# A four-layer graph network: one column of 128 edges per pair of nodes, fetched from the pair's first edge

## The reference

```python
edge_index = stack([src, dst])
h = relu(layernorm(x)); x = x + L0(h)   # relu(batchnorm(sums of (h@W)[src]*dinv[src]*dinv[dst] over dst + own + bias))
h = relu(layernorm(x)); x = x + L1(h)   # q.k attention over the edges of a dst, with e = edge_attr(10)@We
                                        # added to k and v; + h@Wskip; relu, batchnorm
h = relu(layernorm(x)); x = x + L2(h)   # sums over the edges of a src of edge_weight*h[dst]; @W.T + b
h = relu(layernorm(x)); x = x + L3(h)   # sums over the edges of a dst of h[src]; @W; + h@W_self
```

## Time and profile before

| | |
|---|---|
| median of the runs (lowest, highest) | 5445.5 us (5443.48, 5448.52) |
| span of the profiled execution | 5449.7 us |
| TensorE, VectorE, ScalarE, GpSimd busy | 4724.4, 3769.9, 2201.9, 2090.5 us |
| stages: preparation | 0 to 266.6 |
| layer 0's loop | 266.6 to 1120.1 |
| end of layer 0, layer norm, queries | 1120.1 to 1254.8 |
| attention's fetches | 1254.8 to 3533.0 |
| end of layer 1, layer norm | 3533.0 to 3686.6 |
| layer 2 (products of H end) | 3686.6 to 4709.6 |
| layer norm, split, transposes | 4709.6 to 4775.6 |
| layer 3's loop | 4775.6 to 5384.1 |
| the rest | 5384.1 to 5449.7 |

### The profile page before, as it was taken

The page is one execution under the profiler, slowest core; times in us unless marked ns, Lnnn a source line. Parts: engine busy times, 40 slices in busy tenths (PEclk is TensorE's granted clock), DMA queues, the critical chain, the costliest instruction groups (busy, mean ns, idle before and its releaser), DMA issues.

```text
span 5449.7 us, 102910 instructions
## 1 busy us (share of the span) xinstructions
PE 4724.4 (87%) x38199; PEld 3405.6 (62%) x38199; DVE 3769.9 (69%) x6411; ACT 2201.9 (40%) x4109; POOL 2090.5 (38%) x2152
## 2 busy tenths in 40 slices
PE   1299999957888898898889888859999999699997
PEld 0276666735777777777777777725555554356665
DVE  4888888837777777777777777739999997710001
ACT  0166666654555555555555555541222220200000
POOL 4212211006777777777777777700000000001110
PEclk6599999978999999999999999979999999899998
DMA  8156665527888888888888888837888887456664
GB/s 220 64 183 204 215 204 192 178 90 201 216 216 220 217 215 218 220 214 218 217 216 215 212 220 213 212 126 252 296 295 293 299 299 304 180 180 203 208 204 129
DMA packets 1235894, 1154.95 MB, mean 212 GB/s; under 512 B 466847, under 2 KB 1148819, under 8 KB 1206019
## 3 DMA queue, kind: packets, MB, share of 16 engines
q1 hardware_dynamic: 779992, 802.55, 45.9%
q10 hardware_dynamic: 367917, 193.82, 12.6%
q0 software_dynamic: 87488, 151.98, 11.8%
HBM read 691.95 MB, written 468.81 MB: 213 GB/s over the span
## 4 chain that ended last, share of the span: by engine, by line
PE 45%; SPq 18%; POOL 15%; issue 8%; DVE 8%; DMA 3%; ACT 2%; DVEq 0%; POOLq 0%; ACTq 0%
PE psum L1409 44%; POOL G L838 7%; POOL H L838 7%; SPq L629 4%; DVE R L861 4%; SPq L626 3%; SPq L632 3%; SPq L510 2%; SPq L637 2%; DMA H<-local_dst_pairs 1%; ACT H L1727 1%; DVE H L861 1%; SPq L488 1%; SPq L618 1%; POOL R L789 1%
## 5 line engine op out<-in xcount | busy, mean ns | idle before, releaser
L1727 ACT ACTIVATE HT<-psum 98x512 f32<-98x512 f32 (+2 forms) x1527 | 980.0, 680 | 373.5 <-PE psum L1409 307.8
L1409 PE MATMUL psum<-R,HT 128*128 128x384 bf16 x6076 | 1084.9, 326 | 3.8 <-DVEq L1398 3.8
L1727 ACT ACTIVATE H<-psum 128x512 f32<-128x512 f32 (+1 forms) x765 | 455.9, 597 | 1465.5 <-PE psum L1631 774.2
L1409 PE MATMUL psum<-R 128*128 128x98 bf16 (+3 forms) x6858 | 980.4, 281 | 70.3 <-DVE R L861 27.8
L838 POOL DMA_INDIRECT G<-gather_table,cols_pc x908 | 871.1, 959 | 408.2 <-issue 274.2
L838 POOL DMA_INDIRECT H<-gather_table,cols_pc x896 | 858.0, 958 | 273.2 <-issue 270.5
L1409 PE MATMUL psum<-R,ACC 128*98 128x128 bf16 x10752 | 779.0, 221 | 0.0
L1409 PEld LDWEIGHTS psum<-R,HT 128*128 128x128 bf16 x6076 | 566.9, 97 | 327.9 <-DVEq L1398 4.0
L1409 PEld LDWEIGHTS psum<-R,ACC 128*98 128x98 bf16 x10752 | 740.5, 125 | 0.4 <-DVE ACC L861 0.3
L1409 PEld LDWEIGHTS psum<-R 128*128 128x128 bf16 (+1 forms) x6858 | 566.4, 111 | 225.7 <-issue 36.8
L861 DVE TENSOR_TENSOR R<-ACC,G 128x2048 bf16<-128x2048 bf16 x592 | 620.3, 1096 | 117.7 <-PE psum L1409 112.9
(11 more groups left out here) (242 smaller groups left out, 5876.0 us busy)
## 6 DMA issues: line engine op xcount, KB each, us to landing
weighted_blocks<-HT ACTq DMA_DIRECT2D x224, 784.0 KB
adjacency_blocks<-HT SPq DMA_DIRECT2D x74, 1568.0 KB, 5.7
ACC<-weighted_blocks SPq DMA_DIRECT2D x37, 3136.0 KB, 10.9
R<-weighted_blocks SPq DMA_DIRECT2D x37, 3136.0 KB, 10.8
HT<-adjacency_blocks SPq DMA_DIRECT2D x50, 1568.0 KB, 6.6
H<-local_dst_pairs SPq DMA_DIRECT2D x113, 512.0 KB
weighted_blocks<-H SPq DMA_DIRECT2D x72, 784.0 KB
R<-attr_parts SPq DMA_DIRECT2D x451, 99.0 KB
```

Of the source, the lines that this page charges most:

```text
L1409: return nc.tensor.matmul(o, lhs_t, rhs, start=start, stop=stop)
L1727: return nc.scalar.activation(o, a, f, **kw)
```

## The change

Every pair of nodes gets exactly one column of 128 edges, beginning at its first edge. The 3125 pairs take 25 fetches of 128 (`FB`), 3200 columns (`FP`), and 49 blocks (`NBK` = `W`). Block b is window b.

- *Preparation.* GpSimd fetches for every pair the tile in which it begins (25 fetches); VectorE counts there how many destinations are smaller, which gives the first edge; GpSimd fetches 25 rows of destinations and 25 of sources, each starting at this edge, in groups of 4. The 15 destination and 15 source fetches for the attention stand behind them. The DRAM copy `tile_rows` and its two stores are gone. ACT's zero fill of `node_sums` is gone; ScalarE now issues zero fills of the second `node_sums` and of a new tensor after H is ready.
- *Layer 0.* No merge, copy of nodes or accumulation. X is loaded with H from DRAM and multiplied by the degrees in the loop; each block's sums, formed in `sum_parts`, are multiplied by the degrees and added to X (`add_sums`). x is fetched again behind the transposes. Attribute pieces come on every third block. `attention_columns`, `turn_columns`, `copy_columns` and `rows_locb` (forming the attention's index columns) have moved into the first blocks.
- *Layer 1.* All 784 weighted builds stand beside the attention.
- *Layer 2.* No builds, no table store, no fetch of node rows: `send` uses `H[:, b, :]`. HT begins with a load of zeros and VectorE adds into it.
- *Layer 3.* `turn_rows`, `turn_sums` and `last_products` stand in the loop; ScalarE copies (`copy_sums`) and stores the output four windows at a time (`store_output`).
- *Spills.* A pair with more than 128 edges (or reaching too near that) would take a second branch in which GpSimd adds the edges behind one by one. With this data the branch is not taken.

```diff
-    FP = T + FW - 1
-    NBK = (FP + 63) // 64
-    FB = NBK // 2
+    FB = (FW + P - 1) // P
+    FP = FB * P
+    NBK = W
...
+                for b in range(FB):
+                    gather(tile_rows[:, b, :].bitcast(i32), dst_t, first_tile, b).then_inc(s_g[b // 4], 16)
+                pool.wait_ge(s_pad, PADS)
+                for b in range(FB):
+                    if b % 4 == 0:
+                        pool.wait_ge(s_edge, b // 4 + 1)
+                    for o, t in ((fine_dst, dst_t), (fine_src, src_t)):
+                        gather(o[:, b, :].bitcast(i32), t.rearrange("r (e a) -> (r e) a", a=1), first_edge, b).then_inc(s_g[b // 4], 16)
+                for b in range(PB):
+                    gather(rows_dst.bitcast(i32)[:, b, :], dst_t, toff, b).then_inc(s_drow, 16)
+                for b in range(PB):
+                    gather(rows_src.bitcast(i32)[:, b, :], src_t, toff, b).then_inc(s_rows, 16)
...
+            for g in range(FG):
+                step(tt(less, tile_rows[:, of, :].bitcast(i32), node_f[:, of].unsqueeze(2).broadcast_to([P, n, P]), ALU.is_lt))
+                step(reduce(rank[:, of], less))
+                step(v.scalar_tensor_tensor(first_edge[:, of], first_tile_f[:, of], float(P), rank[:, of], ALU.mult, ALU.add))
+                v.sem_inc(s_edge, 1)
...
+            def add_sums(b):
+                v.wait_ge(s_zr, b + 1)
+                if b == 0:
+                    v.wait_ge(s_d, steps[0])
+                v.scalar_tensor_tensor(X[:, b, :], block_sum[0][:, b % 2, :], dinv[:, b:b + 1], X[:, b, :], ALU.mult, ALU.add).then_inc(s_z, 1)
...
+                    if i == 2 and b == 1:
+                        v.wait_ge(s_drow, 16 * PB)
+                        step(tt(rows_locb, rows_dst.bitcast(i32), negw.unsqueeze(2).broadcast_to([P, PB, P]), ALU.add))
+                    if i == 0 and b in (1, 2):
+                        attention_columns(b - 1)
+                    if i == 3 and b == 1:
+                        v.wait_ge(s_sum, 16)
+                        step(tt(X[:, :, :], X[:, :, :], dinv_b, ALU.mult))
...
-                    if u == 4 and b >= 2:
-                        merge(0, b - 2)
-            transposes(0, lambda w: ACC[:, w, 0:F], s_z)
+            transposes(0, lambda w: X[:, w, :], s_z)
...
-                mm(psum[:, 5 + n % 3, 0:k * P], h_node[:, b % 2, :], BW_load[b % 2][:, w0_ * P:(w0_ + k) * P]).then_inc(s_tm, 1)
+                mm(psum[:, 5 + n % 3, 0:k * P], H[:, b, :], BW_load[b % 2][:, w0_ * P:(w0_ + k) * P]).then_inc(s_tm, 1)
             for n in range(NB * NBK):
                 send(n)
-                for m in builds_after(n):
-                    build_weighted(m)
...
+            for b in range(NBK + 3):
                 if b < NBK:
+                    aggregate(1, b, adj3[b % 3], range(W))
+                if b < NB:
+                    turn_rows(b)
+                for g, (w0_, n) in enumerate(BLK):
+                    if w0_ + n + 1 == b:
+                        turn_sums(g)
+                    if w0_ + n + 2 == b:
+                        last_products(g)
```

More of the change, by code:

```diff
@@ L204, in gnn_kernel @@
         starts = accflat[:, 2 * PC:2 * PC + W1F]
[L205 to L206 removed]
+        number, count, total, start, order, order2 = (R2[:, P + k:P + k + 1] for k in range(6))
+        at = P + 6
         attr_s = R2[:, at:at + CH * ED].rearrange("p (c a) -> p c a", a=ED)
@@ L212, in gnn_kernel @@
         cmp_p = R2[:, 0:K1 * PB].rearrange("p (b k) -> p b k", k=K1)
[L216 to L220, removed]
+        fine = sb("fine", [P, 8 * FB])
+        first_tile, first_tile_f, rank, first_edge, pair_f, node_f, value_f = (fine[:, k * FB:(k + 1) * FB] for k in range(7))
@@ L245, in gnn_kernel @@
-        fine_sw = HT[:, 0:FB * P].rearrange("p (b e) -> p b e", e=P)
+        hist, hist_x = (R2[:, at + k * FB:at + (k + 1) * FB] for k in range(2))
+        at += 2 * FB
+        near, beyond = (R2[:, at + k * (PC // HB):at + (k + 1) * (PC // HB)] for k in range(2))
+        at += 2 * (PC // HB)
+        under = R2[:, at:at + 2 * P].bitcast(bf16)
+        at += 2 * P
+        assert at <= 2 * CH * P and K1 * PB <= PB * (FB + P) // 2
+        tile_rows, fine_dst, fine_src = (r1[:, k * FP:(k + 1) * FP].rearrange("p (b e) -> p b e", e=P) for k in range(3))
@@ L1031, in _ @@
-            step(ts(part_i, iota_p[:, :], 1, None, ALU.bitwise_and))
-            step(v.tensor_copy(part, part_i))
-            for k in range(2):
-                step(ts(spread[:, k, :], halfc, 64.0 * k, row[:, 0:1], ALU.add, ALU.is_equal))
-                step(ts(spread[:, 2 + k, :], ones[:, :], 64.0 * k, row[:, 0:1], ALU.mult, ALU.is_equal))
-            v.wait_ge(s_hs, 3)
-            step(v.tensor_copy(step_at, psum[:, 6, 2 * P:2 * P + FB]))
-            step(v.tensor_tensor_scan(step_x, step_at, step_at, 0.0, ALU.add, ALU.bypass))
@@ L1050, in _, with groups @@
-            step(v.tensor_copy(w_first.rearrange(half, h=2), spread_w[:, 2:4, :]))
-            step(v.tensor_copy(node.rearrange(half, h=2), spread_w[:, 0:2, :]))
-            step(tt(mcol[:, :], node, w_first, ALU.subtract))
-            step(ts(mcol[:, :], mcol[:, :], 2.0, part, ALU.mult, ALU.add))
-            step(ts(node, node, 2.0, part, ALU.mult, ALU.add))
-            step(ts(node0[:, :], w_first[0:1, :], 2.0, None, ALU.mult))
-            v.sem_inc(s_fd, 1)
+            def groups(g):
+                n = min(4, FB - 4 * g)
+                return slice(4 * g, 4 * g + n), n
@@ new lines, in _ @@
+            for g in range(FG):
+                of, n = groups(g)
+                at = slice(4 * g * P, (4 * g + n) * P)
+                v.wait_ge(s_ft, 2 * g + 1)
+                step(v.tensor_copy(val_c[:, at], psum[:, g % 2, 0:n * P]))
+                v.sem_inc(s_ftv, 1)
+                step(ts(in_pair[:, at, 0], val_c[:, at], float(W), None, ALU.is_lt))
+                step(v.scalar_tensor_tensor(in_pair[:, at, 1], val_c[:, at], float(J), in_pair[:, at, 0], ALU.is_lt, ALU.subtract))
+                v.sem_inc(s_inp, 1)
@@ L1468, in _ @@
+            for g in range(FG):
+                t.wait_ge(s_fval, g + 1)
                 if g >= 2:
@@ L1676, in send @@
                 if n % NB == 0:
-                    t.wait_ge(s_hx[b % 2], 16 * sum(min(4, FB - 4 * h) for h in range(b % 2, FG, 2)) + 16 * (b // 2 + 1))
                     t.wait_ge(s_al[b % 2], 16 * (b // 2 + 1))
```

805 lines of the change are left out of this document (390 added, 415 removed).

## The result

The changed kernel takes 4438.5 us (median; 4436.1 to 4449.1), against 5444.5 for the kernel before in the same comparison: a ratio of 0.8153, 95% interval 0.8137 to 0.8169. The forecast was 4388, range 4315 to 4460. So the time lies inside the range, and 50 us above the likeliest case, outside that case's own range (4340 to 4430).

A forecast was written before the change was run, and what follows sets the result against it. TensorE was taken to bound layer 0 and layer 3's loop, GpSimd the attention's gathers. Terms -22 - 280 - 18.5 - 499 - 181 - 57 = -1057.5; 5449.7 - 1057.5 - 4.2 = 4388 us, range 4315 to 4460.

The forecast's parts named there:

- a longer preparation: Preparation: one-input passes hold fetches too and seven groups wait for landing, +35 us, 4423; chance 0.12.
- the last sign of the prediction: Layer 0: a TensorE stall per block that 74 blocks with shorter ones did not have would make the forecast wrong.
- 25 x 11.17 and the merges: Layer 0's loop loses 25 of 74 blocks, 279 us, and 49 merges of 0.23, 11 us; whole term -280.
- The 15 attribute stalls stay at 2.1 each: Layer 0's loop: splitting edge attributes still stalls 2.1 us each time, though now every third block.
- Rival 1: Layer 0's loop: VectorE becomes the bound through attribute work on every third block, +55 us, 4443; chance 0.14.
- The preparation: Before layer 0's loop: H ready at 197 instead of 232.4, loop start counted as 244; -22 us.
- the rival with waits for landing: Preparation: each of seven groups of fetches waits 5 to 7 us for landing, +35, 4423; chance 0.12.
- Attention: Layer 1's gathers: GpSimd sets the pace and its 1804 fetches are unchanged; 0, near bound -10 us.
- that rival: Attention: 57 steps without builds run faster, -71 us, 4317; against it, GpSimd waited only 5.2 us for TensorE; chance 0.06.
- Layer 2: Layer 2: 49 blocks at 10.80 us plus about 7.4 at the start, no store or node-row gathers; -499 us.
- Layer 3: Layer 3's loop: 49 blocks at 7.99 us plus 36 for transposes and products moved inside; -181 us.
- the tail: Behind layer 3's loop: of 66 us only the last block's small work and one small store remain; -57 us.

The follow-up runs named there:

- the run with the later copy: Against the changed kernel, ScalarE copies the high part of each attribute group seven eighths of a block later; 4366.6 us, ratio to before 0.8014.
- the experiment: Against the changed kernel, the first layer norm's two two-input passes became 49 one-input instructions each, window by window; 4426.3 us, ratio to before 0.8111.
- the pass in pieces: Layer 2's bias pass cut into 13 pieces, together with the other edits (attribute copy, loop start, layer norm, zero fills), against the changed kernel; 4352.2 us.

## Why the prediction was right, and where its sum was off

- *The number* is right in part by luck. The range was wide upward for VectorE and for a longer preparation, and neither came; what filled it was a wait that the sum had not priced, announced only by the last sign of the prediction, a TensorE stall that 74 blocks did not have. The other six terms came out 26 us shorter than forecast and hid part of it. Without the wait the kernel took 4366.6, 21 below the forecast.
- *Fewer blocks.* 25 x 11.17 and the merges were right: with the wait gone, a plain block comes every 10.96 us (469.72 to 480.68 in the run with the later copy), where it was 11.17 with its merge. The 47 blocks from block 2 took 554.4; 47 x 10.96 and the last aggregation of 8.1 are 523, which leaves 31 for attributes, weights and turned columns, where the forecast had 32 and 2. By the forecast's terms block 2 would have begun at 263 (244, one block of 10.8 and the exposed 8.5) and the stretch would have taken 555. It began at 258 and took 627.8: 5 sooner and 73 longer, which makes the 68.
- *The step that failed* is "The 15 attribute stalls stay at 2.1 each, as they were, though they now come every third block". They became 14 waits of 4.8 and a lower clock, 73 us in all. I had counted engines (ScalarE's, TensorE's and VectorE's work per block) and not the buffer: one copy of the three parts, freed by a store whose 12 us, 8 of them issue, had fitted into a block and three quarters and did not fit into three quarters of one. The rows were to be had: the store's issue and the copy in the trace of before, shown above.
- *Rival 1* (VectorE as the bound, 4443) met the time within 5 us by the wrong mechanism. Its test as I had named it, TensorE waiting for VectorE at the one-hots of every third block, came out negative (6.3 us in all), and VectorE's idle time did not fall to little: it was 136 us of the 628. The test comes out positive only when the attribute work is doubled, or a little (24.2 + 11.2) once the store's wait is gone.
- *The preparation* was right in its end (H at 195.0, forecast 197) and in what held it: the two long fetches cost the 12 that were priced, and the experiment gave back 12.4. Two other terms were off and cancelled: the chain began at 59.97, not at 52, and the short two-input operations cost about 3 us, not 14 (from 59.97 to 168.56 are 108.6, of which 94 are fetches and 12 the long two). GpSimd did not wait between the groups (0.30 of issue ahead of each fetch), so the rival with waits for landing fell. The Trainium skill's "GPSIMD Engine Reference", § 1 Specifications, says that the SBUF interfaces which GpSimd shares with VectorE are contended when VectorE's instruction has two SBUF inputs or runs in a two-port mode. All five long fetches of this trace (6.70 to 7.30, beside two-input passes of 6.69) agree with the first condition, and so do the fetches beside long passes of one input (0.94 or 0.95); of the second no run here tells. The rule's warning was right in kind and too small to turn the change.
- *Attention* 0: -3.7, inside what differs without any edit. Its last 57 steps without builds gave nothing, as that rival's own "against" had it.
- *Layer 2* -499: -512. The rate of 10.80 a block was right (530.2 for 49, 10.8 each), and the loads kept up: TensorE waited 4.4 us for them in all. The exposed start was priced at 7.4; TensorE waited 2.0 us there, as three products run ahead of VectorE, and the pass in pieces gave back 4.6. The joint ahead of it became 19 shorter instead of 13.
- *Layer 3* -181: -187. The products inside cost 31.8 (421.8 less 49 blocks of 7.96, as from 4418.00 to 4425.96) instead of 36; *the tail* was right, 11.4 of it by the stores.

## What to carry to other kernels

When work that ran beside a loop must fit into fewer turns, check each buffer's cycle and not only each engine's load: when it is freed, by which transfer, and how long that transfer's issue and landing take against the new distance to the next writer. A wait on the engine that also empties psum stops TensorE although neither is busy. And a transfer costs what it delays: at the loop's start the two zero fills cost 6 us once the blocks began sooner; inside the loop the fill just ahead of an attribute store cost 10 and the one behind a store nothing; in the gaps between layers both cost nothing that shows.

## What the runs showed of the hardware

- TensorE's granted clock over the loop was 0.93 with 14 stalls of about 5 us in 628 us, 0.89 with 15 of up to 12 us, 0.96 where it waited for VectorE up to 4.0 us at a time, and 1.00 where no wait behind VectorE or ScalarE was over 1.5 us. Behind one stall of 5.5 us it was 0.50 for 4.2 us, and seven products took 2.44 us instead of 1.30. The store's wait of 66.9 us so cost 73.
- 49 short instructions of one input in place of one of two inputs took 3.1 us longer in the first of two passes, and the two passes so changed made the chain of fetches beside them 12.4 us shorter.
- The attention's 1804 fetches took from 2270 to 2295 us in the profiled executions of kernels that have no edit there; GpSimd's waits for TensorE in that time ran from 2.7 (in the shortest) to 31.1 (in the longest). What makes TensorE late was not tried and stays open; the difference is as large as the smaller edits here, which is why these are read by stage.
